# A four-layer graph network in one launch: one list of left-over edges in groups of nine columns, GpSimd's issuing tied to other engines' progress, and layer 3's column numbers in a PSUM bank

## What is computed

```python
x = layernorm(x + L0(x))   # two weighted sums of x[src] over the edges of dst, three branches, attention
x = layernorm(x + L1(x))   # sum, max and mean of edge_attr over the edges of src, then a small MLP
x = layernorm(x + L2(x))   # Gaussian weights from the degrees of src and dst, 4 kernels, mean over dst
x = layernorm(x + L3(x))   # relu(W1 [x_src, x_dst, edge_attr]) summed over dst, W2, then a GRU cell
```

## Time and profile before

| | us |
|---|---|
| median of 3 runs (7647.06 to 7652.19) | 7649.85 |
| span of the profiled execution | 9369.1 |
| PE, PEld, DVE, ACT, POOL busy in it | 5537, 4543, 5345, 1663, 4789 |
| `placing`, profiled, 97 to 3290 | 3193 |
| `layer0_rest`, 3290 to 4290 | 1000 |
| `layer1_scatter`, 4440 to 5462 | 1022 |
| `layer2_edges`, 5872 to 7070 | 1198 |
| `layer3_edges`, 7295 to 9160 | 1865 |
| everything else | 1091 |

### The profile page before, as it was taken

How to read it: one execution, slowest core, us unless ns; L and a number is a source line. 1 busy time by engine, 2 the same in 40 slices (tenths; PEclk the granted TensorE clock), 3 DMA queues, 4 the chain that set the end, 5 groups by cost and what they waited for, 6 DMA issues and landing times. The chain is left out here.

```text
span 9369.1 us, 138875 instructions
## 1 busy us (share of the span) xinstructions
PE 5537.1 (59%) x49076; PEld 4542.6 (48%) x49077; DVE 5345.0 (57%) x9166; ACT 1663.2 (18%) x3235; POOL 4789.4 (51%) x4394
## 2 busy tenths in 40 slices
PE   2555555555555523233455542899996677777777
PEld 1333333333333322223345441899995566666665
DVE  5555655565556533334344455666665677777773
ACT  0111111111111100002111131000002333333333
POOL 3555555555555454550355551455550577667670
PEclk7666676666666666665666675999996788888885
DMA  3222222221222154441100030111110333333330
GB/s 98 77 82 78 73 75 81 78 78 70 81 78 80 40 92 89 88 88 29 42 20 19 20 109 12 26 26 27 27 27 17 106 100 97 95 93 95 95 92 13
DMA packets 392774, 612.74 MB, mean 65 GB/s; under 512 B 158383, under 2 KB 318995, under 8 KB 377363
## 3 DMA queue, kind: packets, MB, share of 16 engines
q1 hardware_dynamic: 240826, 478.03, 16.7%
q0 software_dynamic: 141056, 124.52, 6.4%
q10 hardware_dynamic: 10454, 4.04, 0.2%
HBM read 531.52 MB, written 216.25 MB: 80 GB/s over the span
## 5 line engine op out<-in xcount | busy, mean ns | idle before, releaser
L321 POOL DMA_INDIRECT pay_d<-row,place x1632 | 1719.7, 1054 | 1524.9 <-DVE place L497 947.9
L415 PE MATMUL win<-onehot,val 128*128 128x128 f32 x4998 | 1045.4, 353 | 672.4 <-issue 455.3
L415 PEld LDWEIGHTS win<-onehot,val 128*128 128x128 f32 x4998 | 872.3, 251 | 926.8 <-issue 644.4
L514 DVE TENSOR_TENSOR onehot<-near_dve,drel 128x896 f32<-128x896 f32 x357 | 389.3, 1091 | 1182.2 <-remote 1057.4
L2113 POOL DMA_INDIRECT m_from_src<-from_src_d,m_row x510 | 684.0, 1341 | 628.5 <-issue 375.4
L1712 PE MATMUL g_win<-g_hot,y_part 128*128 128x128 bf16 x14994 | 880.7, 220 | 145.1 <-DVE g_hot L1761 101.1
L1692 POOL DMA_INDIRECT g_x<-xg_d,g_row x510 | 641.5, 1258 | 625.1 <-PE g_win L1712 411.7
L1712 PEld LDWEIGHTS g_win<-g_hot,y_part 128*128 128x128 bf16 x14994 | 857.3, 99 | 166.8 <-DVE g_hot L1761 102.1
L1091 POOL DMA_INDIRECT sorted_d<-s_row,s_place x510 | 494.1, 969 | 531.0 <-DVE s_place L1207 368.5
L672 POOL DMA_INDIRECT r_x<-in_x,r_row x510 | 485.2, 951 | 500.9 <-DMA r_row<-pay_d 351.2
L2116 POOL DMA_INDIRECT m_from_dst<-from_dst_d,m_row x510 | 631.0, 1237 | 160.0 <-issue 155.7
(11 more groups left out here) (410 smaller groups left out, 11491.4 us busy)
## 6 DMA issues: line engine op xcount, KB each, us to landing
m_hot_t<-drow_d SPq DMA_DIRECT2D x52, 1568.0 KB
scan_d<-in_none SPq DMA_DIRECT2D x51, 1034.2 KB
lo_row<-lo_d SPq DMA_DIRECT2D x51, 1024.0 KB
m_grid<-pay_d SPq DMA_DIRECT2D x52, 882.0 KB
pay_d<-in_fill SPq DMA_DIRECT2D x51, 882.0 KB
grid<-pay_d SPq DMA_DIRECT2D x51, 882.0 KB, 3.8
pay_d<-in_fill SPq DMA_DIRECT2D x51, 720.0 KB
row<-in_pay SPq DMA_DIRECT2D x51, 576.0 KB
```

Source lines behind the costliest of these rows:

```text
L321: pool.indirect_dma_start(a["pay_d"][:, :], bass.IndirectOffsetOnAxis(ap=place[j][:, c:c + 1], axis=0), row[j][:, c, :], None).then_inc(ro ...
L415: mm(win[:, :], val[u % 2][:, s, :], onehot[u % 2][:, s, :], start=(u == 0 and s == 0), stop=(u == NS - 1 and s == SUB - 1))
```

## The change

1. **One list.** A secondary row's place is the number of secondary rows ahead of it in the whole graph (`ahead`, carried from block to block). A group is then SR = 1152 rows in a row, SC = 9. A new stage `grouping` reads each group's first and last destination from HBM, and works out the number of windows and each group's first destination (`k.group`), which replaces the block's `k.base` wherever secondary rows are handled. There are still 51 groups a round.
2. **Waits of GpSimd.** In `placing` before columns 20, 23, 26 and 29 on VectorE's `val_ready`; in `layer0_rest` before column 4 on a new semaphore `through`, which PE raises; in `layer1_scatter` before columns 4 and 7 on PE's `bc_ready` and `cum_ready`.
3. **Layer 3.** The column numbers (`k.iota`, `k.steps`) that L2285 and L2307 compare with are copied once into a PSUM bank of VectorE's own. To free that bank, the two `ea_ps` tiles become halves of one bank, and `turn_in` waits for one copy more.

```diff
-SC = 10
+SC = 9
...
+                behind = {20: 1, 23: 3, 26: 4, 29: 5}
...
                     for c in range(CB):
+                        if c in behind and not (isinstance(b, int) and b < 1):
+                            pool.wait_ge(val_ready, (b - 1) * NS + behind[c])
+                            pool.sem_inc(k.pool_steps, 1)
...
-                    v.tensor_copy(k.n_sec[:, at(b)], incl[:, CB - 1:CB])
...
-                    v.scalar_tensor_tensor(out=pos[:, :], in0=pos[:, :], scalar=k.sec_at[:, at(b)], in1=sums[:, 0:CB],
+                    v.scalar_tensor_tensor(out=pos[:, :], in0=pos[:, :], scalar=ahead[:, 0:1], in1=sums[:, 0:CB],
                                            op0=ALU.add, op1=ALU.add)
                     dve.drain()
+                    v.tensor_tensor(ahead[:, :], ahead[:, :], incl[:, CB - 1:CB], ALU.add)
...
+def grouping(nc, z, k, a):
+    G = NR * z.NBK
...
+                for e, r in enumerate((0, SR - 1)):
+                    sp.dma_start(ends[:, e, :, :], rows[:, :, r, AT_DST:AT_DST + 2]).then_inc(ends_in, 16)
...
+                nc.tensor.matmul(first, k.ones[0:1, :], ends_f[:, 0, :], start=True, stop=True).then_inc(first_ready, 1)
...
+                v.tensor_reduce(windows[:, :], steps[:, :], AX, ALU.add)
+                dve.drain()
+                v.tensor_copy(k.counts_i[:, 1:2], windows[:, :])
+                v.tensor_scalar(k.win_at[:, :], k.n_at[:, :], windows[:, 0:1], None, ALU.mult)
+                dve.wait_ge(first_ready, 1)
+                v.tensor_copy(k.group[:, :], first)
...
-                                 sv[bass.ds(b * NR + r, 1)].rearrange("k p w -> (k p) w")).then_inc(row_in[j], 16)
+                                 sv[at(n)].rearrange("n p w -> (n p) w")).then_inc(row_in[j], 16)
...
                     for c in range(SC):
+                        if c == SC // 2:
+                            pool.wait_ge(through, n + 1)
...
+                pe.sem_inc(through, 2)
...
+                    pe.sem_inc(through, 1)
...
                     for c in range(SC):
+                        if c == 4:
+                            pool.wait_ge(bc_ready, n + 2)
+                            pool.sem_inc(k.pool_steps, 1)
+                        if c == 7:
+                            pool.wait_ge(cum_ready, n + 2)
...
-        ea_ps = [ps(f"m_ea_ps{u}", [P, 512]) for u in range(2)]
+        ea_bank = ps("m_ea_ps", [P, 2, 2 * P])
+        ea_ps = [ea_bank[:, u, :] for u in range(2)]
+        near = ps("m_near_dve", [P, 512])
+        numbers, steps = near[:, 0:W], near[:, W:W + WS]
...
-                    pe.wait_ge(copied, n * (2 * NS) + (2 * u + 1 if u else 3))
+                    pe.wait_ge(copied, n * (2 * NS) + (2 * u + 3))
...
-                    v.tensor_tensor(hot[u][:, :, :], k.iota[:, :].unsqueeze(1).to_broadcast([P, SUB, W]),
+                    v.tensor_tensor(hot[u][:, :, :], numbers.unsqueeze(1).to_broadcast([P, SUB, W]),
```

More of the change, by code:

```diff
@@ L203, in _ @@
                 v.tensor_copy(k.base_i[:, :], spans[0:1, :, 0])
[L204 removed]
+                v.tensor_tensor(k.top[:, :], spans[0:1, NBK - 1, 0:1], spans[0:1, NBK - 1, 1:2], ALU.add)
                 v.tensor_tensor(srcf[:, :].rearrange("p (g c) -> p g c", c=CB),
@@ L243, in placing @@
         incl = sb("incl", [P, CB])
+        ahead = sb("sec_ahead", [P, 1])
         pos = sb("pos", [P, CB])
@@ L566, in _ @@
                 v.tensor_copy(k.counts_i[:, 0:1], incl[0:1, NR - 1:NR])
+                dve.drain()
+def grouping(nc, z, k, a):
+    G = NR * z.NBK
+    with ExitStack() as ctx:
+        sb, ps, sem = make(nc, ctx)
+        ends = sb("group_ends", [1, 2, G, 2])
+        ends_f = sb("group_ends_f", [1, 2, G])
+        span = sb("group_span", [1, G])
+        widest = sb("widest", [1, 1])
+        steps = sb("steps", [1, MW])
+        windows = sb("windows_here", [1, 1])
+        first = ps("group_first", [P, 512])[:, 0:G]
+        ends_in, ends_ready, first_ready = sem("group_ends_in"), sem("group_ends_ready"), sem("group_first_ready")
+        rows = a["pay_d"][z.grid_rows:z.grid_rows + z.sec_rows, :].rearrange("(a g r) w -> a g r w", a=1, r=SR)
+        with nc.Block() as block:
+            @block.sync
+            def _(sp):
+                for e, r in enumerate((0, SR - 1)):
+                    sp.dma_start(ends[:, e, :, :], rows[:, :, r, AT_DST:AT_DST + 2]).then_inc(ends_in, 16)
+            @block.tensor
+            def _(pe):
+                pe.wait_ge(ends_ready, 1)
+                nc.tensor.matmul(first, k.ones[0:1, :], ends_f[:, 0, :], start=True, stop=True).then_inc(first_ready, 1)
+            @block.vector
+            def _(dve):
+                v = nc.vector
+                v.tensor_scalar(steps[:, :], k.iota[0:1, 0:MW], float(WS), None, ALU.mult)
+                dve.wait_ge(ends_in, 32)
+                v.tensor_copy(ends_f[:, :, :], ends[:, :, :, 0].bitcast(i32)).then_inc(ends_ready, 1)
+                dve.drain()
+                v.scalar_tensor_tensor(out=span[:, :], in0=ends_f[:, 1, :], scalar=k.top[:, 0:1], in1=ends_f[:, 0, :],
+                                       op0=ALU.min, op1=ALU.subtract)
+                dve.drain()
+                v.tensor_reduce(widest[:, :], span[:, :], AX, ALU.max)
+                dve.drain()
+                v.tensor_scalar(widest[:, :], widest[:, :], 0.0, None, ALU.max)
+                dve.drain()
+                v.tensor_scalar(steps[:, :], steps[:, :], widest[:, 0:1], None, ALU.is_le)
+                dve.drain()
+                v.tensor_reduce(windows[:, :], steps[:, :], AX, ALU.add)
+                dve.drain()
+                v.tensor_copy(k.counts_i[:, 1:2], windows[:, :])
+                v.tensor_scalar(k.win_at[:, :], k.n_at[:, :], windows[:, 0:1], None, ALU.mult)
+                dve.wait_ge(first_ready, 1)
+                v.tensor_copy(k.group[:, :], first)
@@ L2593, in build @@
                     placing(nc, z, k, a)
+                grouping(nc, z, k, a)
                 layer0_rest(nc, z, k, a)
```

63 lines of the change are left out of this document (29 added, 34 removed).

## The result

The changed kernel takes 7384.07 us (median of 4, 7375.11 to 7391.87) beside 7648.45 us of the kernel before (4 runs, 7642.84 to 7652.19): a ratio of 0.9654, 95% interval 0.9641 to 0.9668. The profiled execution has a span of 7385.3 us, so this time the profile and the timed runs are of one kind.

The account below looks back on a forecast made before the run. GpSimd's issuing was taken to bound `placing`, `layer0_rest` and `layer1_scatter`, PE layer 2, and a chain PE, VectorE, ACT layer 3. -64 - 65 - 29 - 6 + 12 = -152 us from 7650 gave 7498, rounded to 7500; range 7410 to 7620.

Parts of the forecast that it names:

- crawl: PE doing matmuls one at a time while GpSimd issues without a pause; claimed the profiled execution's own, 1550 us in three stages.
- waits in `placing`: GpSimd's new waits on VectorE would each be met: 0 us when timed, while the profiled span falls by 1000 or more.
- `layer0_rest`: One gather less a group in this GpSimd-bound stage: 64 us gained, down to 0 if the rings are the bound.
- `layer1_scatter`: One GpSimd issue less a group: 65 us gained, 20 if the handed-on chain is the bound at a lower clock.
- layer 2: PE-bound; four of 40 matmuls of L1725 go: 29 us gained, bounds 20 and 40.
- `grouping`: The new stage's two loads, short VectorE operations and one matmul would cost 12 us, bounds 8 to 25.
- layer 3: PE, VectorE, ACT chain as bound: -20 us for shorter one-hot and matmuls, +14 for the second transpose's wait.
- GpSimd is late there: In layer 3, the bank's faster GpSimd issues were priced 0, with a bound of -80 us if GpSimd is late.
- my own sum: Profiled 9369 us less 1550 of crawl gave 7820; the remaining 170 were put down to profile against timed run.
- the first: GpSimd issues faster in timed runs, so a column costs 0.96 us: 7610 us, chance 0.12.
- The second: The crawl is real in timed runs, and the waits remove part of its 1550 us: 6500 us, chance 0.06.
- The third: The waits in `placing` become the bound, costing 190 us: 7690 us, chance 0.06.

Follow-up runs that it names:

- g1: The kernel before with layer 3's gathers replaced by GpSimd stand-ins, eight iotas of 143 elements a column, ten columns: 7677.5 us, ratio 1.005.
- g2: The kernel before with layer 3's gathers replaced by GpSimd stand-ins, eight iotas of 173 elements a column, ten columns: 7785.35 us, ratio 1.019.
- e10: The kernel before without layer 3's gathers (tiles zeroed once, semaphore raised by GpSimd): 9011.52 us beside 9254.62; layer 3 takes 1612 us.
- kernels e, f and h: Follow-up sets: parts alone or left out, or no layer 3 gathers; too-long stand-ins; list or bank left out. The kernel before beside them: 9198 to 9404 us.
- e4: The kernel before with only the two ea_ps tiles as halves of one bank and one copy more waited for, column numbers in SBUF: ratio 0.9982.
- e5: The whole changed kernel, measured again where the kernel before took 9246.91 us: 8622.78 us, ratio 0.9325.
- e6: The changed kernel without layer 3's bank, beside the kernel before at 9246.91 us: 8564.96 us, ratio 0.9271.
- e9: The kernel before with list and GpSimd's waits, no bank, without layer 3's gathers: 8429.47 us beside 9254.62; layer 3 takes 1625 us.
- e11: The changed kernel without layer 3's gathers: 8441.42 us beside 9254.62 of the kernel before; layer 3 takes 1614 us.

## Why the prediction was right or wrong

| part | forecast, us | measured without a crawl, us |
|---|---|---|
| waits in `placing` | 0 (-30 to +190) | 2311 (g1) and 2316 (g2) to 2314: 0 |
| `layer0_rest` | -64 (-64 to 0) | 687 to 630: -57 |
| `layer1_scatter` | -65 (-65 to -20) | 739 to 675: -64 |
| layer 2 | -29 (-40 to -20) | 1168 to 1140: -28 |
| `grouping` | +12 (+8 to +25) | 2.4 to 9.1 between the stages: +7 |
| layer 3 | -6 (-90 to +40) | 1727 to 1616: -111 |
| sum | -152 | -253; the medians' difference is -264 |

The stages are taken whole here; the stretches shown above cut up to 7 us off their ends. Without layer 3 the forecast was -146 and the measured sum is -142.

- **The failed step is layer 3**, and in it two half-sentences: that the bank "speeds up GpSimd, which waits for PE in layer 3 anyway", price 0, and that the two gathers fewer go "at no gain while PE sets the pace". I had read the waits in a stage that crawled. There PE was slow, a group took 36.5 us, and GpSimd did wait for it (192.0 us, below). Without the crawl the chain takes 31.2 us a group, and GpSimd's ten columns take longer: 10 x (1.34 + 1.24 + 0.60) = 31.8 us even by the crawling trace, 33.4 by the estimate above. GpSimd was the bound, and each of the two edits lifted it: 111 us where I had -6. I had done this sum for three stages and not for the fourth. GpSimd's side of it was in the trace; the chain's 31.2 was not, it took e10. The bound of -80 for "GpSimd is late there" was in the text, without a calculation; it should have reached to the chain, -115.
- **The clue was in my own sum.** 9369 less 1550 us of crawl gave 7820, and I put the 170 us that were left to a difference between profile and timed run. Layer 3's own crawl is as large: 1898 us in the trace, 1727 without it, 171. The trace of the kernel before showed it (engine, what waited, for whom; us in total, times, longest):

```profile
DVE m_hid L2291 <- remote: 148.5, 50, 8.1
...
POOL m_from_src L2113 <- PE m_pre L2149: 192.0, 65, 10.1
POOL m_from_src L2113 <- remote: 61.2, 32, 2.6
```

That the two numbers agree so well is luck, since smaller errors make up for each other: by my subtractions `placing`, `layer0_rest` and `layer1_scatter` without a crawl came to about 2337, 646 and 725 us, where they are 2311, 687 and 739, and layer 2 crawls too, 1208 us against 1168.

- **The crawl isn't the profile's own.** That it was absent from the runs timed at 7648 was right, and so was the waits' price of 0 there. The span did fall by more than 1000 us, 1984, but that was luck: I gave it to the waits, and where both kernels crawl the span falls from 9369 to 8655 us only, while g1, which has no waits, shows no crawl at all. The profile of the changed kernel fell among runs that don't crawl. The reason I gave for the crawl was wrong too: 52 runs of the kernel before beside the kernels e, f and h took 9198 to 9404 us. The Trainium skill ("NOTIFIC — the notification-queue block", "Overflow: three behaviours, one of which stalls the engine") says that producers are held when the block's pipeline is full. All the runs here, with a crawl or without, have a span and a clock on record, and one chip had both kinds; so that records are written can't be the whole cause, and whether they are taken away more slowly at some times no run here shows. What brings a run into this state stays open.
- **Layer 3's chain.** -20 for the shorter one-hot and matmuls and +14 for the second transpose's wait were both read on a path that was not the bound. With the gathers out, the list measured +13 and the bank -11 us, at clocks of 0.93, 0.89 and 0.91: nothing that can be told from the clock's effect. The halves alone (e4) ran 13 us faster than the kernel before, in crawling runs, so the second transpose's wait cost nothing there either. In the changed kernel PE waits 45.7 us for ACT's copies before the transposes, and none any more before the matmul behind them, where e10 has 38.0: the wait has moved, as the prediction said, and little more.
- **Right**: that GpSimd's issuing bounds `layer0_rest` and `layer1_scatter`, so that a column there is worth its issue; layer 2 by its matmuls; VectorE's one-hot equally fast from PSUM (1085 ns after, 1086 in the earlier trace rows); and that the issues of the earlier trace rows stretch beside VectorE's reads of SBUF, so that the bank shortens them. The Trainium skill ("SBUF — State Buffer", "Who interferes with whom") says that a VectorE instruction with two SBUF inputs contends with a GpSimd instruction that reads SBUF, and not with one that only writes it. The drop from 1341 to 1147 ns with the bank alone says that these issues are among what is slowed; whether they read SBUF no run shows.
- **Rivals**: the first (GpSimd issues faster when timed) is refuted by the gaps of 0.30 us and the 1060 ns of L316 in a profiled run of 7385 us, as fast as the timed ones. The second (a real crawl) is true of other runs, where the change gives 6.75% instead of 3.5%. The third: the waits in `placing` are met, 35.5 us in all, and cost nothing.

**Is there a better version?** Where PE crawls, the changed kernel without the bank is faster, 8565 against 8623 us, and layer 3 takes 1819 us with the bank (e5) and 1742 without (e6). My reading is that with shorter issues GpSimd issues more densely and PE crawls more; that wasn't tested. Where PE doesn't crawl, the estimate above and the chains of e9 and e11 (1625 and 1614 us) put that version some 10 us behind, if at all. No version was measured in both.

## What to carry to other kernels

When a profiled execution carries a disturbance that the timed runs lack, take it out of every stage, and then look again at who waits for whom: a wait that was read under the disturbance says nothing of the order without it. A remainder of the sum (170 us here) can be a stage not yet looked at. And compare, stage by stage, each engine's own time for a group with the chain's, even where that engine is seen waiting: some 33.4 against 31.2 us was worth 111 us. Where an engine's issues can't be kept apart from what they set off, stand-ins of the same length show whether its time alone is enough to bind the stage; measure the length that they really take in place, since here each group of them came out 1.8 us longer than planned.

## What the runs showed of the hardware that was not expected

- One kernel has two times, 7641 and 9247 us on the same chip, in all the executions around it. The difference is PE going about one matmul at a time, at the worst, while GpSimd issues indirect DMAs. It doesn't happen beside GpSimd's other work, however dense (stand-ins without a pause: no wait for "remote" in 2290 us, in a run whose `placing` crawls), nor, in the same execution, in a stage whose gathers are left out.
- GpSimd's issue of an indirect DMA depends on what VectorE reads: with VectorE's one-hot input moved from SBUF to PSUM, the mean fell from 1341 and 1237 to 1147 and 996 ns (ten columns, crawling runs; 1369 and 1265 with the rest of that edit alone). It is also longer in runs without a crawl, where VectorE's work is denser: 1150 and 1144 ns against 1061 and 1096 (changed kernel).
- One instruction of VectorE can hold GpSimd up for nearly its whole length: beside L2328 (bf16, in place in SBUF, one tensor input, 1.85 us) an iota took 1.86 us instead of 0.24, and a gather's issue 2.46 us instead of 0.94. Once a group, this is most of the 1.8 us by which the stand-ins' groups exceed their columns.
- PE's granted clock falls as the stage gets longer: 0.93 at 1612 us, 0.92 at 1766, 0.88 at 1870 and 0.81 at 2290 (the kernel before, without gathers and with stand-ins).
